# Probabilities turned by VectorE block transposes and SBUF-to-SBUF transfers instead of TensorE transposes, with new engine orders

## What is computed

```python
q = jnp.einsum('bsd,hpd->bhsp', x, q_w.reshape(H, P, D))
k = jnp.einsum('bsd,hpd->bhsp', x, k_w.reshape(H, P, D))
xv = jnp.einsum('bsd,hedp->bshep', x, v_w.reshape(H, E, D, P))
v = jnp.einsum('bshep,bshe->bhsp', xv, gate_v)
att = jax.nn.softmax(jnp.einsum('bhqp,bhkp->bhqk', q, k) * SCALE, axis=-1)
ctx = jnp.einsum('bhqk,bhkp->bqhp', att, v)
weighted = ctx[:, :, :, None, :] * gate_o[..., None]
out = jnp.einsum('bshep,hepd->bsd', weighted, o_w.reshape(H, E, P, D))
```

## Time and profile before

| | |
|---|---|
| median of 3 runs | 3101.38 us |
| span of the profiled execution | 3102.4 us |
| layer 0 (first to last step, about) | 107 to 2520 us of the span |
| PE busy | 2958.3 us, 95% |
| DVE busy | 2183.4 us, 70% |
| ACT busy | 1926.7 us, 62% |
| POOL busy | 1838.9 us, 59% |

### The profile page before, as it was taken

The page is one execution under the profiler, slowest core; times in us unless marked ns, Lnnn a source line. Parts: engine busy times, 40 slices in busy tenths (PEclk is TensorE's granted clock), DMA queues, the critical chain, the costliest instruction groups (busy, mean ns, idle before and its releaser), DMA issues. The chain is left out here.

```text
span 3102.4 us, 53399 instructions
## 1 busy us (share of the span) xinstructions
PE 2958.3 (95%) x17672; PEld 2071.1 (67%) x17672; DVE 2183.4 (70%) x4152; ACT 1926.7 (62%) x4366; POOL 1838.9 (59%) x2333
## 2 busy tenths in 40 slices
PE   4999999999999999999999999999999987899998
PEld 2666666666666666666666666666667675567675
DVE  7777888877778888777788887777777655235243
ACT  1576666676667666666666666666666743353634
POOL 2466666676666666676766676666666645433330
PEclk7899999999999999999999999999999989899999
DMA  5000001100100011001000110011001011233222
GB/s 171 21 22 23 22 22 33 32 23 26 44 26 22 23 32 33 23 23 37 29 22 22 33 32 23 23 37 29 23 22 40 16 42 44 65 96 104 86 77 87
DMA packets 140048, 124.71 MB, mean 40 GB/s; under 512 B 28662, under 2 KB 122304, under 8 KB 139680
## 3 DMA queue, kind: packets, MB, share of 16 engines
q1 hardware_dynamic: 127312, 88.75, 10.2%
q0 software_dynamic: 10160, 30.17, 3.1%
q10 hardware_dynamic: 2304, 2.36, 0.4%
HBM read 97.47 MB, written 29.28 MB: 41 GB/s over the span
## 5 line engine op out<-in xcount | busy, mean ns | idle before, releaser
L1340 DVE TENSOR_REDUCE m_peaks<-m_ring 128x1 f32<-128x512 f32 x1024 | 636.7, 681 | 95.3 <-PE m_ring L299 95.1
L1072 ACT ACTIVATE m_expA<-m_ring 128x512 f32<-128x512 f32 x1024 | 536.3, 607 | 120.5 <-PE m_ring L372 102.3
L933 POOL TENSOR_TENSOR m_vprod<-m_vprod 128x512 f32<-128x512 f32 x256 | 334.3, 1306 | 451.5 <-DVE m_vprod L1353 327.1
L1043 ACT ACTIVATE m_prob<-m_ring,m_negs 128x512 f32<-128x512 f32 x512 | 350.8, 691 | 285.9 <-DVE m_negs L1388 285.4
L943 POOL TENSOR_TENSOR m_oprod<-m_oprod 128x512 f32<-128x512 f32 x256 | 329.4, 1287 | 258.9 <-ACT m_oprod L1012 255.2
L350 PE MATMUL m_ring<-m_probT,m_vs 128*128 128x256 f32 x2048 | 464.4, 380 | 5.8 <-DVE m_vprod L1353 5.2
L350 PEld LDWEIGHTS m_ring<-m_probT,m_vs 128*128 128x128 f32 x2048 | 386.3, 190 | 68.4 <-issue 13.3
L1378 DVE TENSOR_REDUCE m_negs<-m_ring 128x1 f32<-128x512 f32 x512 | 344.3, 684 | 115.3 <-PE m_ring L105 113.2
L1353 DVE TENSOR_TENSOR m_vprod<-m_ring,m_gate 128x512 f32<-128x512 f32 x512 | 342.2, 687 | 112.4 <-PE m_ring L105 99.5
L1053 ACT ACTIVATE m_probT<-m_ring 128x512 f32<-128x512 f32 x512 | 294.0, 610 | 63.2 <-PE m_ring L338 61.8
L1012 ACT ACTIVATE m_oprod<-m_ring,m_go 128x128 f32<-128x128 f32 x1024 | 292.0, 372 | 34.6 <-PE m_ring L105 23.7
(11 more groups left out here) (322 smaller groups left out, 5558.3 us busy)
## 6 DMA issues: line engine op xcount, KB each, us to landing
m_wraw<-in_v_w SPq DMA_DIRECT2D x32, 512.0 KB, 4.1
m_qf<-q_dram SPq DMA_DIRECT2D x128, 128.0 KB, 2.7
m_wraw<-in_o_w SPq DMA_DIRECT2D x32, 512.0 KB, 4.3
q_dram<-m_kf SPq DMA_DIRECT2D x24, 256.0 KB, 4.4
listed<-in_pad SPq DMA_DIRECT2D x6, 897.0 KB, 11.5
m_xg<-listed SPq DMA_DIRECT2D x39, 138.0 KB
m_rows<-answers SPq DMA_DIRECT2D x8, 512.0 KB, 4.1
sums_dram<-m_sumsT ACTq DMA_DIRECT2D x128, 18.0 KB
```

The source lines that it names most:

```text
L933: vchain(pool.tensor_tensor(vprod[:, 0:512], vprod[:, 0:512], vprod[:, 512:1024], ALU.add))
L1043: act.activation(prob[t % 2][:, c * 512:(c + 1) * 512], ring.home["scores", n, t, c][:, :], ACT.Exp, bias=neg[t % 2], accum_out=den[n % 2] ...
L1072: act.activation(expA[hh][:, c * 512:(c + 1) * 512], ring.home["scT", n, k, hh, c][:, :], ACT.Exp)\
L1340: v.tensor_reduce(peaks[:, t, hh, c:c + 1], ring.home["peaks", n, t, hh, c][:, :], AX.X, ALU.max)\
```

## The change

`turn` and `keep_turned` are gone. In their place DVE's new `turn_probs(n, t)` transposes all 32x32 blocks of a 128x1024 tile of `prob` in one instruction, into `turned`, ordered so that what belongs to one block row of the result is one run of 2 KB for a pair of tiles. SP's new `move_probs(n, g)` then issues 16 DMAs for a pair of tiles; each moves 32 partitions x 2 KB from 32 partitions of `turned` to 32 partitions of `probT` (1 MB in all). `turned` and `probT` are single buffers; before, `probT` was double. `keep_ctx` and `lower_ctx` put the columns, which now come in blocks, back into tile order.

```diff
-        probT = [m.sbuf(f"probT{k}", [P, TPB, 2 * P]) for k in range(2)]
+        probT, turned = m.sbuf("probT", [P, 4, TPB, 64]), m.sbuf("turned", [P, 4, TPB, 2, 32])
...
-                def turn(n, t, h):
...
                 def weigh(n, g):
...
-                    pe.wait_ge(probT_kept, 16 * n + 4 * g + 4)
+                    pe.wait_ge(probs_moved[g % 2], moved(n, g))
                     ps = claim(ring, ("ctx", n, g), ctx_ready, 4 * n + g + 1)
                     for k in range(TPB):
-                        last = pe.matmul(ps[:, 0:2 * P], vs[n % 2][:, k, :], probT[g % 2][:, k, :],
+                        last = pe.matmul(ps[:, 0:2 * P], vs[n % 2][:, k, :], probT[:, :, k, :],
                                          start=(k == 0), stop=(k == TPB - 1))
...
+                def move_probs(n, g):
+                    if n not in steps:
+                        return
+                    sp.wait_ge(probs_turned, 8 * n + 2 * g + 2)
+                    if 4 * n + g >= 1:
+                        sp.wait_ge(ctx_made, 4 * n + g)
+                    for a in range(4):
+                        for b in range(4):
+                            sp.dma_start(probT[32 * b:32 * b + 32, a, :, :].rearrange("p k q -> p (k q)"),
+                                         turned[32 * a:32 * a + 32, b, :, :, :].rearrange("p k t j -> p (k t j)")).then_inc(probs_moved[g % 2], 16)
...
                     if k >= 2:
-                        act.wait_ge(probs_turned, 2 * (k - 2) + c + 1)
+                        act.wait_ge(probs_turned, k - 1)
...
-                def keep_turned(n, t, h):
...
+                def turn_probs(n, t):
+                    if n not in steps:
+                        return
+                    k = TPB * n + t
+                    v.wait_ge(probs_made, 2 * k + 2)
+                    if t % 2 == 0 and k:
+                        v.wait_ge(probs_moved[(k // 2 - 1) % 2], moved(0, k // 2 - 1))
+                    v.transpose(turned[:, :, :, t % 2, :].rearrange("p b k j -> p k b j"),
+                                prob[t % 2][:, :].rearrange("p (k b r) -> p k b r", k=TPB, b=4))\
+                        .then_inc(probs_turned, 1)
```

More of the change, by code:

```diff
@@ L681, in store_queries, with load_queries @@
                         sp.dma_start(q_dram[b % 2][:, rows, q * 512:(q + 1) * 512], kf[:, :]).then_inc(q_stored, 16)
-                def load_queries(n):
-                    if n not in steps:
+                def load_queries(n, first=False):
+                    if n not in steps or n == 0 and not first:
                         return
@@ L693, in load_queries, with load_values @@
                             sp.dma_start(qf[rows, :], q_dram[n // HS % 2][2 * h + hh, :, :]).then_inc(q_loaded, 16)
-                def load_values(n):
+                def load_values(n, first=False):
+                    if n not in steps or n < 2 and not first:
+                        return
                     h = n % HS
@@ L814, in _ @@
                         store_queries(after, s - 5)
[L815 removed]
+                    if i == N0 - 4:
                         load_layer1()
[L817 removed]
+                load_values(0, first=True)
+                sp.dma_start(x[:, TPB:NT, :], tiles[:, TPB:NT, :]).then_inc(x_loaded, 16)
+                sp.wait_ge(eye_ready, 3)
+                for q_of in q_dram:
+                    sp.dma_start(q_of[:, 0:2, :], vprod[0:2 * H0, :]).then_inc(q_stored, 16)
+                    sp.dma_start(q_of[:, 26:32, :], vprod[0:6 * H0, :]).then_inc(q_stored, 16)
+                store_queries(0, 0)
+                store_queries(0, 1)
+                load_queries(0, first=True)
+                load_values(1, first=True)
+                filled, pad = (t.rearrange("(k p r) d -> k p (r d)", k=FILLS, p=P) for t in (listed, a["pad"]))
+                for k in range(FILLS):
+                    sp.dma_start(filled[k], pad[k]).then_inc(xo_stored, 16)
+                for i in range(-5, N0 + 5):
+                    load_queries(i)
+                    move_probs(i - 1, 0)
+                    load_outputs(i - 1)
+                    batch_loads(i - 1)
+                    if i == N0:
+                        load_early_heads()
+                    move_probs(i - 1, 1)
+                    load_values(i + 1)
+                    if i == N0:
+                        load_early_rden()
+                    move_probs(i - 1, 2)
+                    move_probs(i - 1, 3)
                 store_xo(B - 2)
@@ L1228, in _ @@
                 keep_qk()
-                for i in range(-3, N0 + 3):
+                for i in range(-5, N0 + 5):
+                    softmax(i, 4, 1)
                     softmax(i, 5, 0)
                     softmax(i, 5, 1)
-                    keep_ctx(i, 0)
                     exps(i, 4, 0, 0)
```

481 lines of the change are left out of this document (221 added, 260 removed).

## The result

The changed kernel takes 3249.64 us (median of four runs, 3237.98 to 3267.27), the kernel before 3100.9 beside it: 1.0487 of its time, 95% interval 1.0451 to 1.0522. That is 4.9% slower where I forecast 2.4% faster, and outside my range (2955 to 3130). The profiled execution has a span of 3236.0 us against 3102.4 before, so the traces must account for 133.6 us. The medians differ by 15 us more, mostly because the profiled execution is the fastest of the four.

What follows compares the result with a forecast made beforehand. PE bounds layer 0, with DVE close behind. 31 steps x (3.8 allowed by both engines - 1.2 waits) = 81 us off 3102.4, 6 on for the drain: span 3027, median 3026 us; range 2955 to 3130, forecast's own 2985 to 3080.

Steps and rivals of the forecast that it cites:

- 1.2 for waits: Each step: 1.2 us put for waits that newly reach PE as DVE fills up, bounds 0 and 4.
- The chain: From one `weigh` to the next: PE needs 3.6 us for products plus 9.8 for the move, 13.4 us.
- The ends: Last steps: less other work covers 13.4 us from `weigh` to `weigh`, so the drain grows some 6 us (0 to 20).
- the issue of a transfer: SP's queue: 0.44 us each, 16 take 7.1 us, last landing 2.7 us after its issue, 9.8 us a move.
- my own turning point: Move length of 12.3 us, at which the forecast gain of 2.6 us a step would be gone.
- Rival 3: SP's moves into single `probT`: slower by the chain of transfers, 3150 us at a move of 13 us; chance 0.15.
- the third distance: Third of four `weigh`-to-`weigh` distances a step on PE, about 12.8 us, short of 13.4 by 0.6 us.
- Onto PE: 32-row products in broken groups: one more run and six more rounds cost PE 2.8 us a step, bounds 0.6 and 3.2.
- The turns: PE's transposes of probabilities: 16 turns a step, 0.44 us each, removed from PE, 7.0 us a step.
- rival 4: DVE's block transposition makes two passes, 2.4 us each, time 3235 us; chance 0.05.
- rival 2: Nothing gained: each DVE transposition loses 0.49 us, seemingly waiting for POOL, time 3098 us; chance 0.10.
- The floor of 72.1: Step length that DVE and PE would allow, the larger of the two averaged over eight steps, against 75.9 us before.

Runs made afterwards that it cites:

- both relieved: Changed kernel with 4 transfers of 128 partitions a move and DVE transposing 256 of 1024 columns a tile, some work left out: 3056.99 us, 0.9849 of the kernel before.

## Why the prediction was wrong

**Where the 209 us went.** The forecast was a span of 3027, the trace has 3236.0. Steps without the chain: 74.9 us against my 73.3 (72.1 and 1.2 for waits), 31 x 1.6 = 50; what they hold stands below. The chain: 79.6 - 74.9 = 4.7, 31 x 4.7 = 146. The ends: 20 us in place of 6, of which 11 are also there with four transfers. 50 + 146 + 14 = 210.

**The step that failed: the issue of a transfer.** "SP issues 4 loads of 32 partitions in 1.77 us ..., 0.44 each ...; 16 take 7.1 us". I carried a row for a load from DRAM over to a transfer from SBUF to SBUF. (The rival's "64 KB each 0.44 us" misreads it too: these loads carry 128 KB.) A transfer within SBUF takes 0.59 us as a record and 0.63 to 0.66 start to start. By my sum, sixteen prices and a landing, a move is 12.3 us, not 9.8, and my own turning point was 12.3. The sum counts one issue too many, since a landing is reckoned from the start of its issue: in the trace a move takes 11.8 us. I had no upper end for this term in the sum, only a rival. The time stands on this step: with four issues in place of sixteen the kernel was 165 us faster, and 0.6% faster than the one before.

**Rival 3 was the right mechanism at too low a price.** At a move of 12.3 us it said that the gain is gone, so a time near 3102; it went 134 us beyond. Three things were missing. First, the gain that it ate into was 1.0 us a step, not 2.6. Second, it reckoned from `weigh` to `weigh` 3.6 us and the move, which is 15.4 with the measured 11.8; the chain took 16.2 and 16.8, for 4.3 and 4.7 us pass between the start of a `weigh` and the first issue. So the third distance grew by 1.5 us (to 16.2) from a base of 14.7, and the second by 0.9. The fourth grew by 1.9 too, though it has over 10 us to spare if only `weigh` counts: there the chain seems to run through softmax, transposition, the load of queries behind it on SP's queue (ACT waited 282.9 us for `m_qf`, 164.6 with four transfers, 92.6 before) and ACT's order. "SP's own queue is passed by `load_queries` ... and cost nothing unless a move is late": moves were late. Third, PE's clock. These are two windows of 5 us and PE's row in the second:

```profile
882.50:887.50 5.00, 5.00 (x29) 4.03 (x26) 3.52 (x9) 2.35 (x6) 4.17 (x7) 1.00 0.46 107
...
892.50:897.50 5.00, 5.00 (x18) 4.09 (x17) 3.01 (x5) 3.31 (x8) 0.54 (x1) 0.71 0.11 38
```

```profile
891.41 5.41 PE L368 MATMUL m_ring<-m_probT,m_vs 128*128 128x256 f32 x16 [2.67 <-DMA m_probT<-m_turned]
896.47 0.58 PE L130 MATMUL m_ring<-m_wos,m_ctxT 128*128 128x512 f32 x1
```

After an idle of 2.67 us the granted clock is 0.71 in the window, between the levels of 2.4 and 1.2 GHz, and the `weigh` takes 5.06 us to the next start (3.53 is the mean before). The Trainium skill (TensorE: Matmul & The Clock Gate, section "Why this matters for your kernels") warns that a wait for DMA inside the loop lets the clock fall; the trace agrees, with 0.71 behind this wait. In layer 0, 14 of 124 `weigh`s begin 2.5 to 4.4 us after PE's start before, where 0.23 is usual, and the mean `weigh` is 3.77 us: 124 x 0.24 = 30 us, all of it in the 15 that meet the lower level. The waits themselves are 90.1 us there (of the 101.7). The remaining 26 of the 146 us are 14 of idle time ahead of other products and 12 of slower work. The 30 us are not all the chain's, though. With four transfers the clock falls too, on other products, for a cause that I didn't settle: it stands at its lower level for 61 us of the 31 steps, of which PE is busy 56; after the change for 92 and 83, before it for 7 and 7. At half speed that is an estimated 14 us of work from four transfers to sixteen.

**Onto PE: 3.2 us for 2.8, and a clock that I had at nothing.** The count of runs and rounds was right, and the price nearly. A run of five took 0.22 to 0.54 us more than a group of four, where I had 0.36 for the extra round, and one of seven 0.94, which I had counted as one extra round too. The 1.6 us that the step without the chain is over my 73.3 lie elsewhere for the most part. Idle time of PE grew by 1.6 us a step (0.7 to 2.3), just what I had allowed (72.1 less the 71.7 of PE alone, and 1.2). The turns gave 0.3 less than the 7.0, the rounds took 0.4 more. Some 0.8 us is the clock, by an estimate: 56 busy us at the lower level for 7, at half speed, over 31 steps. My sum had no term for the clock.

**What was right.** The turns came off nearly in full: PE's start-to-start account shows 6.7 us a step for them before and none after (forecast 7.0). The transposition takes 1235 ns (forecast 1.25), so rival 4 fell. No transposition is stretched to the 641 ns pattern of the earlier trace rows; the instruction that had it takes 301 ns now, and rival 2 fell. POOL is as busy as before (1842 us for 1839), so what stretched that instruction is open. `weigh` with columns in runs of 64 costs nothing: 382 ns a record with four transfers, 380 before. DVE had 66.9 us a step, ACT 43.8; I said 67 to 71 and near 42. The floor of 72.1 (the rows give 72.0) was not reached by any run: with both relieved the step is still 74.2 us, and PE idles 2.0 of it. What I said would show rival 3 (a wait of `weigh` for DMA of over 60 us) was there, at 101.7.

## What to carry to other kernels

Before an engine's work is replaced by many transfers, cost the chain as issues x price + landing, with a price from the same kind of transfer or with half as much again as the upper end, and compare it with the bound engine's shortest distance between two users of the tile; it costs little below that length and much above it. A single-buffered tile between two engines in fixed orders is such a place. And an order of work that keeps PE full is a solution for banks, queues and clock together: shifting one item by 2 us, or healing five rounds, cost 58 to 138 us here, part of it by waits and part by a lower granted clock.

## What was unexpected of the hardware

- The issue of a transfer between partitions of SBUF holds SP's queue for 0.63 to 0.66 us whether it carries 16 or 64 KB (0.60 for 256 KB over 128 partitions), 0.61 us on ACT as a record; four stores of 4 runs in each of 32 partitions 2.85 together, as records 0.3, 0.4, 0.7 and 1.3; one load of 1 MB from DRAM 0.34. What sets the price is open.
- A run of five 32-row products takes 0.65 us or 0.97 for the same count of rounds, without idle time in it; why is open.
- `weigh` takes 5.06 us in place of 3.53 in the row above, where PE had idled 2.67 us, and the granted clock over layer 0 (130 to 2440 us) is 0.98 after and 1.00 before, 0.96 with the shifted `weigh` and 0.88 with issues on ACT, where PE also idles most (349 us of the 31 steps, 177 after). How much of a loss is the clock and how much the wait has to be read apart: PE's busy time for the same records, and its idle time.
